# A recommender tower on one core: the second half's gathers wait for the first half's gram

## Chip, core and metric

The kernel runs on one core of a Trainium2 chip. The metric is the device time of one execution in microseconds (us), as the median of several runs; lower is better. The engines are TensorE (PE in the profile; PEld is its weight load), VectorE (DVE), ScalarE (ACT), GpSimd (POOL) and SyncE (SP). DMAs are issued from the queues of SP, ACT and POOL.

## What is computed

For each of 2048 samples, 27 embedding rows of 128 values are looked up in 27 tables, all pairwise dot products of them are taken (351 pairs), and the result goes through three layers with the sample's `r_bottom_mlp_out`:

```python
e = jnp.stack([tbl_0[ids[:, 0]], tbl_1[ids[:, 1]], ..., tbl_26[ids[:, 26]]], axis=1)
interactions = jnp.einsum('bfd,bgd->bfg', e, e)
x = interactions.reshape(B, F * F)[:, TRIL_IDX]      # the 351 entries below the diagonal
z = jnp.concatenate([r_bottom_mlp_out, x], axis=1)
h = jnp.concatenate([z, r_bottom_mlp_out], axis=1)
h = jnp.maximum(h @ W_top1 + b_top1, 0.0)            # 607 -> 512
h = jnp.maximum(h @ W_top2 + b_top2, 0.0)            # 512 -> 256
y = h @ W_top3                                       # 256 -> 1
```

The tables have 1000, 1250, 12500 or (one of them) 125000 rows; everything is float32.

## The kernel before

The samples are cut into 16 **halves** of 128 (`HALVES`), two of which make one tile for the layers. The 27 features of a half come in two ways.

**Ten small tables are looked up on TensorE.** They lie in SBUF, split into a high and a low part (ScalarE L415, VectorE L624, from stages that SP loads at L337). VectorE compares the ids with row numbers and makes one-hot masks (L583, L587), and TensorE multiplies table chunks by masks (L687). One look-up serves up to four halves; the pairs of tables in `OWN` take turns, so that the look-ups behind a half have 32 or 52 matmuls. The results are copied to `eH` (L424, L600) and placed in `eT` (L438).

**Seventeen tables are gathered.** GpSimd issues one indirect DMA for each table and half (L311): 128 rows of 512 bytes into `rows`, which has space for two halves. They are in five groups of 4, 4, 3, 3 and 3 (`GROUPS`, `NG` = 5). Halves 0, 1 and 2 have a sixth, the extra group (`EXTRA`, L322): 2, 2 and 1 gathers that stand in for small tables whose look-up comes too late. TensorE waits for a group's semaphore, transposes its tables (L706), and ScalarE and VectorE copy them into `eT` (L432, L608).

**The gram.** When all groups of half h are in `eT`, TensorE forms the pairwise products with 128 small matmuls (L723) in four sets (`SETS`) over three banks. ScalarE and VectorE copy them to `pairs` (L468, L618), and SP moves them to `x` (L360), from where TensorE takes them in layer 1 (L742, L746); layer 2 is L778, layer 3 L788.

**Order on TensorE**, written out by hand: the front (look-ups 0 to 3 between the transposes of half 0), gram 0, then the look-ups behind it; then for each half h from 1: its transposes, a part of the layers of an earlier tile (two blocks of layer 1 in even halves, layer 2 in odd ones), gram h, the look-ups behind gram h, and in even halves the other two blocks of layer 1. An instruction that waits holds everything behind it on its engine.

**Order on GpSimd**: it waits for the ids, then goes through the halves and, within one, the groups; the extra group of a half stands behind its five. From half 2 on, each group waits until the same group of half h - 2 has been transposed (L304), since its space is used again, and the first group also waits for the end of gram h - 2 (L308). Half 0 and half 1 have neither wait. `gram_full` is counted up by the last matmul of each set; set n of all sets uses bank n % 3.

SP, in its own order: the ids, the small tables (each stage again when the split of an earlier one has been made), hot ids, the weights (L385 to L392), and then for each half the loads for the layers. ScalarE waits for the weights (L519) before it copies the first pairs.

Of the kernel before, what the change touches and what calls it, by code (L numbers as in the profile page):

```python
# [39 lines left out]
SETS = HALF // SET  # L40
# [29 lines left out]
def used(n, b):  # L70

    return (n - b + BANKS - 1) // BANKS
# [53 lines left out]
def transpose_fill(h, g):  # L126
    return NUMBER["transpose", h, g]
# [18 lines left out]
def build(nc, tables, idx_d, hot_ids_d, bottom_d, w1_d, wa_d, wb_d, b1_d, w2_d, b2_d, w3_d, ident_d, rowid_d, out_d):  # L146
# [6 lines left out]
    with ctx:  # L153
# [65 lines left out]
        def rows_of(h, g):  # L219
            first, size = GROUPS[g]  # L220
            return rows[:, h % 2, first * D:(first + size) * D]
# [6 lines left out]
        def extra_row(h, k):  # L228
            at = (h % 2 * len(LATE) + list(LATE).index(k)) * D
            return h1[:, 2:4, :].rearrange("p m s -> p (m s)")[:, at:at + D]  # L230
# [21 lines left out]
        def looked_up(n, k):  # L252

            _, _, wide = LOOKUPS[n]
            first = (WINDOW - wide) * HALF if n < FRONT else 0
            return eH[:, k, first:first + wide * HALF], col_bank[lookup_fill(n, k) % BANKS][:, 0:wide * HALF]
# [10 lines left out]
        def x_block(h, r):  # L267

            (i, n), row = BLOCKS[r], BLOCK_ROW[r]
            c = max(0, 1 - i)  # L270
            return x[row:row + n, h // 2 % 2, h % 2, c * HALF:X_CHUNKS * HALF], \
                pairs[0:n, (i + c - 1) * HALF:(i + X_CHUNKS - 1) * HALF]

        def layer1_out(u, m):

            if u == TILES:
                return (*col_bank, gram_bank[1].rearrange("p q g -> p (q g)"))[m][:, 0:HALF]
            _, at, size = unit_columns(u)
            return mlp_bank[m // 2][:, m % 2, at:at + size]

        def layer2_out(u, m):
            if u == TILES:
                return gram_bank[2].rearrange("p q g -> p (q g)")[:, m * HALF:(m + 1) * HALF]
            _, at, size = unit_columns(u)
            return mlp_bank[0][:, m, at:at + size]
# [9 lines left out]
        @block.gpsimd  # L295
        def _(pool):
            pool.wait_ge(idx_loaded, 16)
            for h in range(HALVES):
                for g, (first, size) in enumerate(GROUPS):
                    before = h * NG + g - RING  # L300
                    if before >= 0:

                        n = transpose_fill(before // NG, before % NG)
                        pool.wait_ge(col_full[n % BANKS], n // BANKS + 1)  # L304
                    if h >= 2 and g == 0:

                        last = (h - 1) * SETS - 1
                        pool.wait_ge(gram_full[last % BANKS], last // BANKS + 1)  # L308
                    for i in range(size):
                        f = first + i  # L310
                        pool.indirect_dma_start(  # L311
                            out=rows_of(h, g)[:, i * D:(i + 1) * D], out_offset=None, in_=tables[GATHERED_TABLES[f]],
                            in_offset=bass.IndirectOffsetOnAxis(ap=idx[:, h * GATHERED + f:h * GATHERED + f + 1], axis=0),
                        ).then_inc(gathered[(h * NG + g) % RING], 16)
                if h < len(EXTRA):
                    if h >= 2:

                        n = transpose_fill(h - 2, NG)
                        pool.wait_ge(col_full[n % BANKS], n // BANKS + 1)
                    for k in EXTRA[h]:  # L320
                        at = HALVES * GATHERED + EXTRA_IDS.index((h, k))
                        pool.indirect_dma_start(  # L322
                            out=extra_row(h, k), out_offset=None, in_=tables[HOT_TABLES[k]],
                            in_offset=bass.IndirectOffsetOnAxis(ap=idx[:, at:at + 1], axis=0),
                        ).then_inc(extra_gathered[h], 16)
            for b in range(BANKS):
                pool.wait_ge(gram_copied[b], STRIPS * used(HALVES * SETS, b))
            for r in range(2, len(BLOCKS), 3):
                out, src = x_block(LAST, r)
                pool.dma_start(out, src).then_inc(last_x_loaded, 16)  # L330
# [555 lines left out]
```

## Time and profile before

| | us |
|---|---|
| median of 3 timed runs | 412.73 (412.5 to 413.49) |
| span of the profiled execution | 563.8 |
| own time of the profiled execution beside its span | none is given |
| mean granted clock of TensorE | 0.845 of full speed |
| TensorE busy / GpSimd busy (profiled) | 395.0 / 292.0 |
| VectorE / ScalarE busy (profiled) | 231.8 / 156.7 |
| moved by DMA | 40.50 MB, mean 72 GB/s |

One execution was profiled, and it was 151 us longer than a timed run. Its rows show durations of single instructions, their order and what released them. In a row, "idle before <-X" is the time that the engine stood before this instruction and what ended the wait; "issue" is time in which the engine waited for nothing that the profile shows; "remote" or "another core or an unknown queue" is a release that the profile can't attribute. PEclk is the clock granted to TensorE, as a share of 2.4 GHz. DMA share is the mean busy share of the core's 16 DMA engines.

### The profile page before, as it was taken

Reading aid. Unit: us, or ns where it says so; the run is one execution under the profiler, and the core shown is the slowest. Engines: PE = TensorE matmul, PEld = TensorE weight load, DVE = VectorE, ACT = ScalarE, POOL = GpSimd, SP = SyncE. Lnnn points to the kernel's source line nnn. Section 1 sums busy time; section 2 is a strip of 40 time slices with the busy share of each in tenths; the row PEclk is TensorE's granted clock in tenths of the full one; section 3 lists DMA queues with packets and bytes.
Section 4 is the critical chain, followed back from the end, with each engine's and each line's share of the span. In section 5 each row is a group of like instructions: output and inputs, shape, how many; then the busy total and the mean of one; then the engine's idle time right before and its main releaser. Section 6 shows DMA issues by size and latency. Waiting matters only on the chain.

```text
span 563.8 us, 9147 instructions
## 1 busy us (share of the span) xinstructions
PE 395.0 (70%) x3669; PEld 336.8 (60%) x3669; DVE 231.8 (41%) x430; ACT 156.7 (28%) x337; POOL 292.0 (52%) x284
## 2 busy tenths in 40 slices
PE   1620868397979578688939587797979490924987
PEld 1520756285868467576737376676857390823977
DVE  3530667073836143373617052472716050422430
ACT  3200543021424142324115042322215041401433
POOL 6776007656574747374735737373746656172010
PEclk9975898688989979699969879697979785885999
DMA  8761272122331312041411212140413111030000
GB/s 212 193 170 47 79 185 70 48 84 66 93 86 29 99 35 74 23 118 34 145 28 62 76 33 72 24 117 24 131 37 75 48 53 51 6 95 19 16 8 9
DMA packets 20737, 40.50 MB, mean 72 GB/s; under 512 B 7128, under 2 KB 11428, under 8 KB 20696
## 3 DMA queue, kind: packets, MB, share of 16 engines
q1 hardware_dynamic: 11674, 21.64, 14.1%
q0 software_dynamic: 8960, 18.22, 12.8%
q8 instruction: 29, 0.48, 0.3%
q14 instruction: 12, 0.10, 0.1%
q10 hardware_dynamic: 62, 0.06, 0.1%
HBM read 36.81 MB, written 0.01 MB: 65 GB/s over the span
## 4 chain that ended last, share of the span: by engine, by line
PE 51%; issue 18%; another core or an unknown queue 11%; DVE 8%; DVEq 3%; ACT 3%; DMA 3%; SPq 1%; ACTq 0%
PE col_bank L687 17%; PE gram_bank L723 15%; PE mlp_bank L778 6%; PE mlp_bank L746 6%; DVE mask L583 4%; PE col_bank L706 4%; DVEq L590 3%; PE mlp_bank L742 2%; DMA b<-in_b 2%; DVE mask L587 2%; ACT eT L438 1%; DMA pairs<-in_tbl 1%; DVE parts L624 1%; DVE eT L608 1%
## 5 line engine op out<-in xcount | busy, mean ns | idle before, releaser
L311 POOL DMA_INDIRECT rows<-in_tbl,idx x272 | 285.5, 1050 | 219.2 <-PE gram_bank L723 138.1
L687 PE MATMUL col_bank<-mask,parts 125*128 125x512 f32 (+3 forms) x768 | 168.0, 381 | 21.8 <-DVE parts L624 12.2
L687 PEld LDWEIGHTS col_bank<-mask,parts 125*128 125x128 f32 x768 | 139.8, 204 | 45.0 <-DVE parts L624 12.1
L583 DVE TENSOR_SCALAR mask<-hot_i,rowid 125x1024 fp32r<-125x1024 int32 (+3 forms) x152 | 103.9, 684 | 65.0 <-remote 30.6
L723 PE MATMUL gram_bank<-eT 128*58 128x52 f32 x2048 | 87.2, 244 | 59.6 <-issue 54.0
L723 PEld LDWEIGHTS gram_bank<-eT 128*58 128x58 f32 x2048 | 78.5, 160 | 71.3 <-issue 67.1
L618 DVE COPY pairs<-gram_bank 26x208 f32<-26x208 f32 x128 | 46.7, 365 | 159.4 <-remote 91.5
L706 PE MATMUL col_bank<-ident,rows 128*128 128x128 f32 x272 | 41.7, 293 | 82.5 <-issue 30.5
L468 ACT ACTIVATE pairs<-gram_bank 26x208 f32<-26x208 f32 x128 | 44.5, 348 | 153.0 <-remote 84.6
L706 PEld LDWEIGHTS col_bank<-ident,rows 128*128 128x128 f32 x272 | 32.4, 149 | 90.7 <-issue 88.4
L424 ACT ACTIVATE eH<-col_bank 128x512 f32<-128x512 f32 (+3 forms) x30 | 15.3, 516 | 148.4 <-issue 59.6
L608 DVE COPY eT<-col_bank 128x384 f32<-128x384 f32 (+2 forms) x42 | 25.1, 611 | 67.3 <-remote 47.0
L746 PE MATMUL mlp_bank<-x,w 126*128 126x256 f32 (+3 forms) x192 | 48.1, 389 | 0.0
L438 ACT ACTIVATE eT<-eH 128x256 f32<-128x256 f32 (+1 forms) x64 | 43.3, 788 | 16.0 <-issue 9.0
L746 PEld LDWEIGHTS mlp_bank<-x,w 126*128 126x128 f32 (+1 forms) x192 | 37.4, 203 | 5.7
L587 DVE TENSOR_SCALAR mask<-hot_i,rowid 125x512 fp32r<-125x512 int32 (+2 forms) x80 | 33.5, 461 | 5.6 <-PE col_bank L687 1.6
L778 PE MATMUL mlp_bank<-h,w 128*128 128x256 f32 (+1 forms) x128 | 35.7, 445 | 0.0
L778 PEld LDWEIGHTS mlp_bank<-h,w 128*128 128x128 f32 x128 | 28.9, 241 | 5.0
L432 ACT ACTIVATE eT<-col_bank 128x384 f32<-128x384 f32 (+2 forms) x41 | 21.7, 553 | 28.6 <-remote 20.2
L742 PE MATMUL mlp_bank<-bottom,w 128*128 128x256 f32 (+1 forms) x64 | 20.6, 405 | 0.0
L477 ACT ACTIVATE h<-mlp_bank,b 128x256 f32<-128x256 f32 (+1 forms) x32 | 13.0, 458 | 26.6 <-remote 20.3
L330 POOL DMA_DIRECT2D x<-pairs x3 | 1.6, 532 | 36.1 <-DVE pairs L618 36.1
(34 smaller groups left out, 83.9 us busy)
## 6 DMA issues: line engine op xcount, KB each, us to landing
hot_i<-in_hot_ids SPq DMA_DIRECT2D x13, 512.0 KB
rows<-in_tbl,idx POOLq DMA_INDIRECT x272
pairs<-in_tbl SPq DMA_DIRECT2D x8, 448.0 KB
hot_i<-in_hot_ids SPq DMA_DIRECT2D x8, 256.0 KB
pairs<-in_tbl SPq DMA_DIRECT2D x2, 560.0 KB
bottom<-in_bottom SPq DMA_DIRECT2D x8, 128.0 KB
hot_i<-in_hot_ids SPq DMA_DIRECT2D x2, 384.0 KB
x<-pairs SPq DMA_DIRECT2D x16, 39.0 KB
```

Of the source, the lines that this page charges most:

```text
L311: pool.indirect_dma_start(out=rows_of(h, g)[:, i * D:(i + 1) * D], out_offset=None, in_=tables[GATHERED_TABLES[f]], in_offset=bass.Indirec ...
L438: return nc.scalar.activation(eT[:, :, first:last].rearrange("p s f -> p f s"), eH[:, first:last, at:at + HALF], ACT.Copy)
L468: last = nc.scalar.activation(pairs_of(s, 1, j), gram_of(n % BANKS, 1, j), ACT.Copy)
L583: last = nc.vector.tensor_scalar(mask[0:ROWS, entry % MASKS, 0:2 * size], ids, row_of(ks[0], c), None, ALU.is_equal)
L587: last = nc.vector.tensor_scalar(mask[0:ROWS, entry % MASKS, i * size:(i + 1) * size], ids, row_of(ks[0], 2 * c + i), None, ALU.is_equal)
L618: last = nc.vector.tensor_copy(pairs_of(s, 0, j), gram_of(n % BANKS, 0, j))
L687: last = nc.tensor.matmul(col_bank[fill % BANKS][:, 0:size], parts[k][0:ROWS, part, c * D:(c + 1) * D], mask[0:ROWS, entry % MASKS, at:at ...
L706: last = nc.tensor.transpose(col_bank[fill % BANKS][:, i * HALF:(i + 1) * HALF], src, ident[:, :])
L723: last = nc.tensor.matmul(gram_bank[n % BANKS][COLUMNS * t:COLUMNS * t + GRAM_ROWS, q, 0:PACK * (F - 1)], eT[:, a:a + PACK, :].rearrange(" ...
L742: nc.tensor.matmul(layer1_out(u, m), w1[:, X_CHUNKS, m * 128:(m + 1) * 128], bottom[:, buf, at:at + size], start=True, stop=False)
L746: last = nc.tensor.matmul(layer1_out(u, m).rearrange("p (h s) -> p h s", s=HALF), w1[0:k, c, m * 128:(m + 1) * 128], x[0:k, buf, at // HAL ...
L778: last = nc.tensor.matmul(layer2_out(u, m), w2[:, c, m * 128:(m + 1) * 128], h1[:, c, at:at + size], start=(c == 0), stop=(c == N1 // 128 ...
```

## The change

GpSimd's wait for a gram stands ahead of half 1 too. For half 1 it is the last set of gram 0; for half 2, which waited for gram 0 before, it is the same wait again, and for the later halves nothing changes. No DMA, no size and no other engine's instructions are changed.

```diff
--- before.py
+++ after.py
@@ -302,9 +302,9 @@
 
                         n = transpose_fill(before // NG, before % NG)
                         pool.wait_ge(col_full[n % BANKS], n // BANKS + 1)
-                    if h >= 2 and g == 0:
-
-                        last = (h - 1) * SETS - 1
+                    if h >= 1 and g == 0:
+
+                        last = max(1, h - 1) * SETS - 1
                         pool.wait_ge(gram_full[last % BANKS], last // BANKS + 1)
                     for i in range(size):
                         f = first + i
```

## Rows read from the trace of the kernel before

**Rows 1.** The page's head: span and instructions.

```profile
span 563.8 us, 9147 instructions
```

**Rows 2.** The page's chain that ended last: shares of the span by engine.

```profile
PE 51%; issue 18%; another core or an unknown queue 11%; DVE 8%; DVEq 3%; ACT 3%; DMA 3%; SPq 1%; ACTq 0%
```

**Rows 3.** Waits, 31 to 54 us: waited for: total, times, longest.

```profile
ACT eH L424 <- issue: 28.8, 1, 28.8
DVE mask L583 <- issue: 9.2, 2, 6.4
```

**Rows 4.** Timeline, TensorE, gram 1: start, us, what [idle before <-releaser].

```profile
102.31 0.34 PE L723 MATMUL gram_bank<-eT 128*58 128x52 f32 x4 [1.11 <-issue]
...
112.26 3.44 PE L723 MATMUL gram_bank<-eT 128*58 128x52 f32 x63 [0.45 <-issue]
```

**Rows 5.** Chain, halves 9, 10 and one gram: start, us, what.

```profile
331.31 7.48 PE col_bank L687 x32
...
347.90 0.93 PE gram_bank L723 x29
...
361.67 12.15 PE col_bank L687 x52
...
381.45 0.46 PE gram_bank L723 x12
...
420.87 3.55 PE gram_bank L723 x128
```

**Rows 6.** Chain, front: shares over 34.6 to 58.05 us; gram 0's end.

```profile
by line: another core or an unknown queue 44.8%; issue 43.2%; DVE mask L583 13.9%; DVEq L590 0.8%
...
82.59 1.84 PE gram_bank L723 x32
```

**Rows 7.** Stretches to gram 0's end: engines busy, PEclk, DMA share, GB/s.

```profile
0.00:28.80 28.80, 11.04 (x51) 10.92 (x52) 12.34 (x20) 7.84 (x9) 20.38 (x23) 1.00 0.79 200
28.80:53.40 24.60, 3.31 (x19) 2.97 (x18) 5.48 (x7) 0.00 (x0) 18.81 (x20) 0.61 0.48 119
53.40:84.40 31.00, 22.20 (x208) 19.30 (x208) 18.03 (x25) 13.90 (x26) 0.03 (x1) 0.83 0.48 122
```

**Rows 8.** Timeline, GpSimd: first and last gather of halves 1, 2, 3.

```profile
29.14 0.94 POOL L311 DMA_INDIRECT rows<-in_tbl,idx  x1 [0.30 <-issue]
...
52.49 0.94 POOL L322 DMA_INDIRECT h<-in_tbl,idx  x1 [0.30 <-issue]
85.22 1.63 POOL L311 DMA_INDIRECT rows<-in_tbl,idx  x1 [31.79 <-PE gram_bank L723]
...
108.92 0.94 POOL L322 DMA_INDIRECT h<-in_tbl,idx  x1 [0.30 <-issue]
116.48 0.94 POOL L311 DMA_INDIRECT rows<-in_tbl,idx  x1 [6.62 <-PE gram_bank L723]
...
138.38 0.94 POOL L311 DMA_INDIRECT rows<-in_tbl,idx  x1 [0.30 <-issue]
```

**Rows 9.** Waits over the whole span, GpSimd's.

```profile
POOL rows L311 <- PE gram_bank L723: 138.1, 14, 31.8
```

**Rows 10.** DMA issues: KB each, median us to landing.

```profile
x<-pairs POOLq DMA_DIRECT2D x1, 16.5 KB, 2.0
```

**Rows 11.** Chain near the end.

```profile
527.71 5.95 PE col_bank L687 x52
...
538.49 0.87 PE col_bank L706 x6
```

**Rows 12.** Timeline, TensorE, from gram 0 to gram 1.

```profile
84.36 9.62 PE L687 MATMUL col_bank<-mask,parts 125*128 125x512 f32 x32
...
97.65 0.38 PE L706 MATMUL col_bank<-ident,h 128*128 128x128 f32 x2
98.66 0.55 PE L723 MATMUL gram_bank<-eT 128*58 128x52 f32 x13 [0.63 <-DVE eT L608]
```

**Rows 13.** The stretch with TensorE's long stop.

```profile
32.00:54.00 22.00, 0.11 (x2) 0.00 (x0) 3.97 (x6) 0.27 (x1) 16.56 (x17) 0.55 0.51 126
```

## The prediction, made before the change was run

> **What bounds the kernel now.** Read first how far the profile can be trusted in length. The page gives a span of 563.8 us [rows 1], while the timed runs have a median of 412.73 us, 151 us less; no own time of the profiled execution is given beside its span. The chain that ended last names the surplus: "issue" holds 18% and "another core or an unknown queue" 11% of the span [rows 2], and 29% of 563.8 us is 164 us, close to 151. So I take nearly all of that idle time to belong to the profiled execution alone. What it looks like: in the first stretch ScalarE stood still for 28.8 us and VectorE for 9.2 us in two waits, with nothing named but "issue" [rows 3], and in the gram of half 1 TensorE paused for about 1 us every few matmuls while GpSimd gathered, then ran 63 of them in 3.44 us once it had stopped [rows 4]. The same 128 matmuls without these pauses take 3.55 us [rows 5].
>
> Next, take them out of the front. I call T the end of gram 0: 82.59 + 1.84 = 84.4 us in the profile. Between 34.6 and 58.05 us the chain has 44.8% + 43.2% of such pieces, which of 23.45 us is 20.6 us [rows 6]. That puts T in a timed run near 63.8 us. The DMA rates by stretch are the check [rows 7]: 28.8 x 200 + 24.6 x 119 + 31.0 x 122 thousand bytes are 12.5 MB by T, which at the first stretch's 200 GB/s are 62 us. The front is thus close to what the queues moved at their fastest.
>
> Then the steady part, and here two engines are almost level. **GpSimd**: one gather is 0.94 us with 0.30 us before it, and up to 1.63 us beside VectorE's masks [rows 8]. Eighteen of them take 85.22 to 109.86 us, 24.6 us; seventeen 116.48 to 139.32 us, 22.8 us, so 23.1 us to the start of the next set if it never waits. **TensorE** without pauses: half 9 is 16.6 us from the first of its 32 look-up matmuls (331.31) to the gram's start (347.90), with 3.55 us of gram 20.1 us; half 10, with 52 look-ups, is 19.8 us (361.67 to 381.45), with the gram 23.3 us [rows 5]; the mean is 21.7 us. So a gather set (23.1) is longer than TensorE's half (21.7). In the profile GpSimd looks slack, waiting 138.1 us for the gram in 14 waits [rows 9], but only because TensorE's halves were stretched to some 31 us there.
>
> Does GpSimd's row of gathers give the timed total? From T: 0.8 us to wake (84.43 to 85.22), 24.9 us for half 2's, 13 x 23.1 = 300.3 us for halves 3 to 15, about 2.0 us for the last to land (a GpSimd DMA of 16.5 KB landed in 2.0 us [rows 10]), and 25.3 us from the last transposes at 538.5 us to the end of the span [rows 11]. Together 353.3 us; with T = 63.8 that is 417 us, 1% above the median. The same by TensorE: 17.8 us to the end of gram 1 (gram 1 began 14.2 us after T [rows 12], and 3.55), 13 x 21.7 = 282 us, and 36.1 us from 527.7 to the end [rows 11], 336 us in all, 400 us with T. The gathers fit better, so I take GpSimd as the bound after gram 0, with between 0 and some 10 us of slack.
>
> **The change part by part.** Nothing is removed. The 17 gathers of half 1 and, behind them on the same engine, the 2 of its extra group now wait for gram 0; halves 2 and later wait for what they waited for. Before, the 19 began at 29.14 us and ended at 53.43 us, and GpSimd was idle for 31.8 us from there to gram 0 [rows 8]. Queued behind the waiting instruction are all later gathers, and nothing else; nobody but TensorE's transposes waits for them. SP's queue isn't touched.
>
> First term, **the gathers added behind T**: 19 x 24.9 / 18 = 26.3 us. Everything of GpSimd after T moves back by this.
>
> Second, how it shows at TensorE. Its order is fixed: 32 look-ups, transposes of half 1, gram 1. The gram began at T + 14.2 us. It now begins when the nineteenth gather has landed and been transposed and copied: 0.8 + 26.3 + 2.0 + about 1.3 (from the extra group's transposes, after 97.4, to the gram at 98.66 us [rows 12]) = T + 30.4 us, 16.2 us late. Half 2 waits again: its 18 gathers end at 0.8 + 26.3 + 24.9 = 52.0, land at 54, while TensorE, free of gram 1 at 34, has 12.2 us of look-ups [rows 5] and stands from 46 to 54. Before, gram 1 ended at 17.8 and the look-ups at 30, so that transposing began there and ended at 33: half 2 is 21 us late. From then on the lag can only grow, because 23.1 is more than 21.7: up to the full 26.3 us if GpSimd was the bound before, and no less than these 16 to 21 us if it wasn't. So the loss lies between 16 (only gram 1's delay) and 26; I take 26.3 less 2 us for slack, since the sum for GpSimd was over the median and leaves little: **+24.3 us**.
>
> By the Trainium skill ("DMA: Bandwidth & Descriptors", section on the anatomy of one SWDGE DMA) a DMA from GpSimd has some 2.0 us of fixed cost, most of it waiting for the write's receipt. The nearest row here is the closing DMA's 2.0 us, and agrees [rows 10].
>
> Third, **the front gets lighter**. The 19 gathers move 64 KB each (128 rows of 512 B), 1.25 MB, which at 200 GB/s are 6.2 us of the queues' time. If the queues alone set T, it falls by 6.2; if the chain of table load, split, mask and look-up sets it, by 0, since those gathers stand on no step of that chain and the DMA share was 0.48 while they ran [rows 7]. I take **-3 us**.
>
> Fourth, TensorE now idles about 15 us before gram 1 and 8 us before half 2's transposes. After 22 us without a matmul its granted clock was 0.55 of 2.4 GHz over 32 to 54 us [rows 13], where it had been 1.00 before [rows 7]: part of that time at 1.2 GHz. Gram 1 and the 12.2 us of look-ups behind it may cost up to 6 us more at half clock, but behind them TensorE waits 8 us for half 2's gathers anyway. So 0, and +3 at most if the second idle slows half 2 too and GpSimd isn't the bound.
>
> **Sum**: +24.3 - 3 + 0 = +21.3 us. 412.7 + 21.3 = **434.0 us**.
>
> **The rivals.** (1) *Cheap delay.* Outside the profile a gather takes nearer 1.0 us than 1.3 us, because its 0.30 us gap or its contention is the profile's. Then 19 cost 19 us, gram 1 begins at 0.8 + 19 + 2.0 + 1.3 = 23.1, 8.9 us late, half 2's 18 land at 39.8 against look-ups ending near 38.9, and a set of 17 us never binds again: +10 with -3 is 420 us. Against it: the gap is 0.30 us at every gather, long before other engines are busy, and TensorE alone gives only 400 us. (2) *Full price or more.* GpSimd was the bound without slack and the front gives nothing: +26.3, with the clock's +3, 442 us. (3) *The other side, faster: the gathers hold up the front.* VectorE, ScalarE and TensorE stood from about 32 to 53.4 us, and ScalarE's wait of 28.8 us ended, by the rows, as the last of the gathers that the change moves had been made [rows 3, 8]. If that stop is real in part in timed runs, moving them frees it. By the Trainium skill ("Runtime: NRT & Kernel Launch", section on instruction fetch) each engine's sequencer fetches its instructions over its own DMA queue, mostly hidden; the profile lists such queues, but no row here shows a fetch that was late. Its price: up to 20.6 us of front [rows 6] against +24.3 us, and it decides for faster from the point where more than the loss is freed, that is with a loss at its lower end of 16: 412.7 + 16 - 20.6 = 408 us. Against it: with a front of 84 us the timed total would leave 328 us for a rest that takes 336 by TensorE alone. (4) *Nothing happens*: the wait is passed at once. Against it: GpSimd gets there at about 28.8 us and gram 0 ends at 84.4 in the profile [rows 6, 8]. A time unchanged would need 19 gathers that are hidden beside the look-ups, which is 9.6 us of cover for 26.3 [rows 12].
>
> **How the numbers follow.** The forecast, between 424 and 439 us: 0.64. Cheap delay, 416 to 424: 0.15. Full price, 439 to 445: 0.10. Front freed: 0.08, of which 0.05 comes out faster by over 0.3%, 0.02 within it. Nothing happens: 0.03, within it. A difference of 0.3% (1.2 us) is about what a measurement of this kernel can tell from none. The range goes from 418 us, with most of the cheap case, to 441 us. Faster 0.05, same 0.05, slower 0.90.
>
> **What would show it.** In the profile of the changed kernel GpSimd stands from about 28.8 us to the end of gram 0, then issues 37 gathers without a pause, half 1's first. If the stops in the profile go with gathers, TensorE's and ScalarE's stop after 32 us is shorter there and gram 0 ends well before 84 us, which by itself says little of the timed runs. The transposes of half 1 come at the gathers' pace, the first pieces of wait naming the DMA or GpSimd, and gram 1 begins some 30 us behind gram 0. I'm wrong if gram 1 follows gram 0 within 20 us, if GpSimd has long waits for the gram in a run whose halves are as short as the timed ones, or if T is far from 64 us in timed runs.

## The result, and the profile after

| | before | changed |
|---|---|---|
| median of the timed runs, us | 412.62 (411.54 to 413.49, 4 runs) | 433.65 (433.18 to 434.73, 4 runs) |
| ratio, 95% interval | | 1.051 (1.0484 to 1.0536) |
| span of the profiled execution, us | 563.8 | 431.4 |

The change costs 21.0 us, 5.1%. The profile of before, at 563.8 us, shows a condition with stops, in which the kernel before took about 575 us in one later set of 17 runs too; the timed runs of this table were free of it. So the kernel before was profiled once more (the first experiment below), at 410.3 us, and the comparison is made with that.

The waits on GpSimd of the changed kernel, over the whole span (waited for: us in total, times, longest), answer [rows 9]:

```profile
POOL rows L311 <- PE gram_bank L723: 25.8, 4, 24.9
```

and its timeline answers [rows 8]: the first gather of half 1, the last of its extra group, the first of half 2, the last of half 2's group and the last of all.

```profile
55.45 1.29 POOL L311 DMA_INDIRECT rows<-in_tbl,idx  x1 [24.88 <-PE gram_bank L723]
...
80.42 0.95 POOL L322 DMA_INDIRECT h<-in_tbl,idx  x1 [0.30 <-issue]
81.67 0.95 POOL L311 DMA_INDIRECT rows<-in_tbl,idx  x1 [0.30 <-issue]
...
105.05 0.95 POOL L322 DMA_INDIRECT h<-in_tbl,idx  x1 [0.30 <-issue]
...
403.00 0.95 POOL L311 DMA_INDIRECT rows<-in_tbl,idx  x1 [0.30 <-issue]
```

GpSimd stands 24.9 us for the end of gram 0 and then issues its 258 remaining gathers in one row, 347.6 us from start to start: 1.35 us each. What TensorE does meanwhile is seen in its own timeline of the changed kernel, which answers [rows 12]:

```profile
53.33 1.84 PE L723 MATMUL gram_bank<-eT 128*58 128x52 f32 x32 [4.17 <-ACT pairs L468]
55.10 9.45 PE L687 MATMUL col_bank<-mask,parts 125*128 125x512 f32 x32
64.39 0.60 PE L706 MATMUL col_bank<-ident,rows 128*128 128x128 f32 x4
69.14 0.96 PE L706 MATMUL col_bank<-ident,rows 128*128 128x128 f32 x4 [4.15 <-DMA rows<-in_tbl,idx]
72.90 0.90 PE L706 MATMUL col_bank<-ident,rows 128*128 128x128 f32 x3 [2.80 <-DMA rows<-in_tbl,idx]
...
84.18 4.65 PE L723 MATMUL gram_bank<-eT 128*58 128x52 f32 x128 [0.63 <-issue]
...
114.32 3.62 PE L723 MATMUL gram_bank<-eT 128*58 128x52 f32 x128
```

From the second group on, the transposes of half 1 come one group at a time, each released by a gather's landing, and gram 1 begins at 84.18, 29 us after gram 0's end at 55.2. The page's chain that ended last, which answers [rows 2], now has GpSimd in it with 30%:

```profile
PE 43%; POOL 30%; issue 11%; DMA 6%; DVE 4%; DVEq 2%; SPq 2%; ACT 1%; ACTq 0%; POOLq 0%
```

### The profile page after: what moved, and what is told of

Same layout as the page of the kernel before. It is cut to its first block, busy times and chain, and to the rows that moved or that the text cites. A ratio compares the mean times of both kernels' runs of the same rounds, so it can differ in the third digit from the quotient of the medians.

```text
span 431.4 us, 9147 instructions
## 1 busy us (share of the span) xinstructions
PE 364.3 (84%) x3669; PEld 310.2 (72%) x3669; DVE 231.0 (54%) x430; ACT 156.6 (36%) x337; POOL 293.8 (68%) x284
## 4 chain that ended last, share of the span: by engine, by line
PE 43%; POOL 30%; issue 11%; DMA 6%; DVE 4%; DVEq 2%; SPq 2%; ACT 1%; ACTq 0%; POOLq 0%
POOL rows L311 29%; PE col_bank L687 15%; PE mlp_bank L746 8%; PE gram_bank L723 8%; PE mlp_bank L778 4%; PE mlp_bank L742 3%; PE col_bank L706 3%; DMA rows<-in_tbl,idx 3%; DVE mask L583 3%; DVEq L590 2%; DMA b<-in_b 2%; DMA pairs<-in_tbl 1%; PE mlp_bank L788 1%; POOL h L322 1%; DVE mask L587 1%
## 5 line engine op out<-in xcount | busy, mean ns | idle before, releaser
L687 PE MATMUL col_bank<-mask,parts 125*128 125x512 f32 (+3 forms) x768 | 164.7, 375 | 16.3 <-DVE mask L583 16.3
L687 PEld LDWEIGHTS col_bank<-mask,parts 125*128 125x128 f32 x768 | 136.3, 199 | 39.3 <-DVE parts L624 14.8
L468 ACT ACTIVATE pairs<-gram_bank 26x208 f32<-26x208 f32 x128 | 44.3, 346 | 93.0 <-PE gram_bank L723 76.5
L723 PEld LDWEIGHTS gram_bank<-eT 128*58 128x58 f32 x2048 | 57.8, 136 | 11.9 <-issue 7.6
L723 PE MATMUL gram_bank<-eT 128*58 128x52 f32 x2048 | 60.0, 220 | 6.4 <-ACT pairs L468 4.2
L746 PE MATMUL mlp_bank<-x,w 126*128 126x256 f32 (+3 forms) x192 | 52.1, 413 | 0.0
L746 PEld LDWEIGHTS mlp_bank<-x,w 126*128 126x128 f32 (+1 forms) x192 | 41.0, 222 | 7.4
L778 PE MATMUL mlp_bank<-h,w 128*128 128x256 f32 (+1 forms) x128 | 27.4, 367 | 0.0
L778 PEld LDWEIGHTS mlp_bank<-h,w 128*128 128x128 f32 x128 | 22.6, 190 | 2.5
L742 PE MATMUL mlp_bank<-bottom,w 128*128 128x256 f32 (+1 forms) x64 | 23.5, 455 | 0.0
L624 DVE TENSOR_TENSOR parts<-pairs,parts 125x1024 fp32r<-125x1024 f32 (+1 forms) x10 | 12.5, 1276 | 11.2 <-ACT parts L415 10.8
```

The costliest lines, as they stand in the source:

```text
L468: last = nc.scalar.activation(pairs_of(s, 1, j), gram_of(n % BANKS, 1, j), ACT.Copy)
L687: last = nc.tensor.matmul(col_bank[fill % BANKS][:, 0:size], parts[k][0:ROWS, part, c * D:(c + 1) * D], mask[0:ROWS, entry % MASKS, at:at ...
L723: last = nc.tensor.matmul(gram_bank[n % BANKS][COLUMNS * t:COLUMNS * t + GRAM_ROWS, q, 0:PACK * (F - 1)], eT[:, a:a + PACK, :].rearrange(" ...
L742: nc.tensor.matmul(layer1_out(u, m), w1[:, X_CHUNKS, m * 128:(m + 1) * 128], bottom[:, buf, at:at + size], start=True, stop=False)
L746: last = nc.tensor.matmul(layer1_out(u, m).rearrange("p (h s) -> p h s", s=HALF), w1[0:k, c, m * 128:(m + 1) * 128], x[0:k, buf, at // HAL ...
L778: last = nc.tensor.matmul(layer2_out(u, m), w2[:, c, m * 128:(m + 1) * 128], h1[:, c, at:at + size], start=(c == 0), stop=(c == N1 // 128 ...
```

## The experiments

Times of experiments stand beside a kernel before that ran on the same chip; ratios are to that.

**1. The kernel before, once more** (no edit).

> The kernel before, unchanged, profiled once more: the first profile was 151 us longer than a timed run, this one is wanted without those stops. Theory (after gram 0 GpSimd's gathers are the bound): gram 0 ends near 59.6 us, some 4 us later than in the changed kernel, GpSimd's 239 gathers of halves 2 to 15 then follow each other with hardly a wait for a gram (under 5 us in all behind the first), and the span is about 410. Rival (TensorE is the bound in the kernel before, and only the transposes' waiting costs in the changed one): GpSimd waits for the gram in most halves, 10 us or more in sum behind the first, and gram 0 ends earlier than 59.

Measured: 412.3 us, span 410.3. Its timeline of TensorE, from gram 0 to gram 2:

```profile
47.87 2.77 PE L723 MATMUL gram_bank<-eT 128*58 128x52 f32 x96 [2.05 <-ACT eT L438]
57.34 1.85 PE L723 MATMUL gram_bank<-eT 128*58 128x52 f32 x32 [6.70 <-ACT pairs L468]
59.11 8.44 PE L687 MATMUL col_bank<-mask,parts 125*128 125x512 f32 x32
...
72.30 3.62 PE L723 MATMUL gram_bank<-eT 128*58 128x52 f32 x128 [0.63 <-DVE eT L608]
...
97.95 3.62 PE L723 MATMUL gram_bank<-eT 128*58 128x52 f32 x128
```

and of GpSimd, the last gather of half 1's extra group, the first of half 2 and the last of all:

```profile
55.97 0.94 POOL L322 DMA_INDIRECT h<-in_tbl,idx  x1 [0.30 <-issue]
59.97 1.62 POOL L311 DMA_INDIRECT rows<-in_tbl,idx  x1 [3.06 <-PE gram_bank L723]
...
382.72 0.95 POOL L311 DMA_INDIRECT rows<-in_tbl,idx  x1 [0.30 <-issue]
```

Gram 0 ends at 59.2 us, 4.0 us later than in the changed kernel, and none of the long stops of [rows 3, 4] is there. GpSimd's whole wait for grams is 4.0 us, 3.06 of it for gram 0: the 138.1 us of [rows 9] came from the stops on TensorE. The 239 gathers from half 2 on take 322.8 us from start to start, 1.36 us each. So GpSimd's row runs without a break in both kernels, and the last gather begins at 382.72 before and 403.00 after, 20.3 us apart.

The chain that ended last alone would not have shown this. In this profile of the kernel before it names TensorE, and GpSimd with 6% only:

```profile
PE 66%; DVE 9%; DMA 7%; POOL 6%; issue 4%; DVEq 3%; SPq 2%; ACT 2%; ACTq 0%
```

With two engines this close, a chain that passes from one to the other says little about which of them sets the time; experiment 5 tries it.

**2 and 3. Moving fewer gathers behind gram 0.** In the second only the two of the extra group wait, in the third the wait stands ahead of half 1's fourth group (8 gathers behind it).

```diff
# experiment 2, ahead of the loop over EXTRA[h]
+                    if h == 1:
+                        last = SETS - 1
+                        pool.wait_ge(gram_full[last % BANKS], last // BANKS + 1)
# experiment 3
-                    if h >= 2 and g == 0:
+                    if h >= 2 and g == 0 or h == 1 and g == 3:
-                        last = (h - 1) * SETS - 1
+                        last = max(1, h - 1) * SETS - 1
```

> Only the two gathers of half 1's extra group wait for gram 0; half 1's 17 go early as before. Theory (each gather moved behind gram 0 adds its 1.35 us, less its share of the front, 0.23 us): 2 x 1.12 = +2.2 us, 414.8 us. Rival (a few gathers behind gram 0 are hidden by the 9.6 us of look-ups there): 412.6 us, no change.

Measured: 415.06 us beside 413.58, ratio 1.0042 (1.0024 to 1.006), that is +1.0 to +2.5 us.

> The wait stands ahead of half 1's fourth group: 11 gathers go early, 6 and the 2 extra ones wait for gram 0. Theory: 8 x 1.12 = +9.0 us, 421.6 us. Rival (hidden by the look-ups behind gram 0): the eighth lands at 0.3 + 10.8 + 3 = 14 us behind gram 0, when TensorE's transposes reach it anyway, so 413 to 414 us.

Measured: 422.28 us, ratio 1.0201 (1.0165 to 1.0237), +6.8 to +9.8 us. With 2, 8 and 19 gathers moved the cost is about 1.7, 8.3 and 21.0 us, 0.9 to 1.1 us each, so the look-ups behind gram 0 hide nothing of them. The timeline of GpSimd in the third, first gather behind the wait and last of all:

```profile
57.51 1.29 POOL L311 DMA_INDIRECT rows<-in_tbl,idx  x1 [13.08 <-PE gram_bank L723]
...
391.90 0.94 POOL L311 DMA_INDIRECT rows<-in_tbl,idx  x1 [0.30 <-issue]
```

The last gather begins 9.2 us later than in the kernel before.

**4. No gram waits at all.**

```diff
-                    if h >= 2 and g == 0:
-
-                        last = (h - 1) * SETS - 1
-                        pool.wait_ge(gram_full[last % BANKS], last // BANKS + 1)
```

> GpSimd's wait for a gram is taken out of all halves; a group still waits until the same group two halves earlier has been transposed. Theory: half 2's gathers follow half 1's at about 54 us and no longer wait for gram 0 near 59.6, so the row of gathers moves forward by about 5 us: 407 to 408 us. Rival (TensorE is the bound): no change, 412.6 us, or slower, since these gathers then run beside the loads of the weights that gram 0 waits for.

Measured: 411.18 us beside 413.58, ratio 0.994 (0.9911 to 0.9969): faster by 1 to 4 us, less than forecast. The expectation had the end of half 1's gathers from [rows 8], 53.4 us; in the profile of experiment 1, without stops, these gathers run beside a busier VectorE and DMA (DMA share 0.86 from 28.8 us to gram 0's end, where [rows 7] have 0.48), and end at 56.9 us. So only 2 to 3 us of wait were there to be had: half 2's first gather begins at 57.77 in place of 59.97 us, the last of all at 380.95 in place of 382.72.

**5 and 6. Fourteen gathers fewer**, in the kernel before (5) and in the changed one (6). The last table of the fifth group isn't gathered from half 2 on, so one feature keeps the rows of halves 0 and 1.

```diff
-                    for i in range(size):
+                    for i in range(size - 1 if h >= 2 and g == NG - 1 else size):
# and in gathered_count
-        return 16 * sum(GROUPS[k % NG][1] for k in range(n % RING, n + 1, RING))
+        return 16 * sum(GROUPS[k % NG][1] - (k // NG >= 2 and k % NG == NG - 1) for k in range(n % RING, n + 1, RING))
```

> The kernel before with one gather fewer in each half from half 2 on (14 in all): the last table of the fifth group keeps its old rows, so the features of one table are not those of its ids. TensorE waited 11.4 us for gathers in the clean profile of the kernel before. Theory (GpSimd's row is the bound, TensorE close behind): the 14 gathers are worth 14 x 1.35 = 18.9 us, of which only TensorE's 11.4 us can be had, so 401 to 403 us. Rival (TensorE's chain sets the time before the change): 412.6 us, hardly a change.

Measured: 396.8 us beside 413.07, ratio 0.9594 (0.9545 to 0.9643), span 395.1. That is 16.3 us off, more than the 11.4 us that TensorE had waited. The 11.4 us were read from the wrong rows. A transpose begins with its weight load, and it is the weight loads that stand longest for a gather; in the kernel before, profiled again (waited for: us in total, times, longest), they have 14.5 + 1.2 = 15.7 us, near the 16.3:

```profile
PEld col_bank L706 <- DMA rows<-in_tbl,idx: 14.5, 9, 3.1
...
PEld col_bank L706 <- DMA h<-in_tbl,idx: 1.2, 1, 1.2
```

In experiment 5 all that is left of them is one row:

```profile
PEld col_bank L706 <- DMA h<-in_tbl,idx: 0.2, 1, 0.2
```

> The same 14 gathers left out of the changed kernel. Theory: there GpSimd's row has 26 us more behind gram 0 and stays the bound throughout, so nearly all of the 18.9 us comes off: 433.7 - 18.9 = 414.8 us. Rival (the change costs its time once, at gram 1 and half 2, and TensorE's chain rules from there): most of the 21 us stays over the kernel before with the same gathers left out, which gives 430 us if that one is at 412, and anything above 420 speaks for it.

Measured: 417.26 us, ratio 1.0092 (1.0056 to 1.0128); by the ratios (1.051 - 1.0092) that is 17.2 us under the changed kernel, where 18.9 were forecast. Its last gather begins at 385.95 in place of 403.00 us, 17.1 us earlier. Here TensorE still waits for gathers (us in total, times, longest):

```profile
PEld col_bank L706 <- DMA rows<-in_tbl,idx: 21.3, 8, 4.9
PE col_bank L706 <- DMA rows<-in_tbl,idx: 18.8, 7, 4.6
```

So gathers are what the time behind gram 0 is made of, in both kernels. Once they are fewer, TensorE bounds the one from before, at 396.8 us, with GpSimd close behind (its last gather begins 16.0 us earlier and its row still has hardly a break), and GpSimd still bounds the changed one. The rival that the change costs once, at gram 1, and that TensorE rules from there, wanted over 420 and is out.

**7. GpSimd idle in the front instead of behind it.** Half 1's gathers wait for the transposes of half 0's extra group.

```diff
+                    if h == 1 and g == 0:
+                        n = transpose_fill(0, NG)
+                        pool.wait_ge(col_full[n % BANKS], n // BANKS + 1)
```

> Half 1's gathers wait, but for an earlier event: the transposes of half 0's extra group, near 38 us, where GpSimd comes by at 30 us. Its idle time of 7 to 8 us is then in the front. Theory (time off GpSimd's row costs as soon as it uses up the 3.1 us that GpSimd waited for gram 0): half 2's gathers begin at 63 to 64.5 us in place of 60.0, so +3 to +4.5 us: 415.5 to 417 us. Rival (gathers cost only if they are issued behind gram 0, where look-ups and masks run): 412.6 us, or less by the front's relief.

Measured: 418.01 us beside 413.07, ratio 1.0119 (1.0094 to 1.0144), +4.9 us. The timeline of GpSimd, the first gather of half 1 and the first of half 2:

```profile
37.70 1.17 POOL L314 DMA_INDIRECT rows<-in_tbl,idx  x1 [9.92 <-PE col_bank L709]
...
66.35 1.51 POOL L314 DMA_INDIRECT rows<-in_tbl,idx  x1 [0.30 <-issue]
```

The idle time was 9.9 us rather than 7 to 8, and half 2's row begins 6.4 us later than before and its last gather 4.2 us later (386.93 us), so the numbers are over the forecast by the same cause. Idle time of GpSimd in the front costs too, beyond the 3 us that it had to spare. The rival of the expectation, that only gathers issued behind gram 0 cost, isn't excluded by this run: gram 0 ends at 57.9 us here, and five of half 1's gathers begin behind it, which at the 0.9 to 1.1 us of experiments 2 and 3 would be 4.5 to 5.5 us. In a row without gaps the two ways of counting give nearly the same sum.

**8 to 12. Gram 0 earlier.** ScalarE waits for the weights ahead of its first copies of pairs, which hold up gram 0's last set (57.34 above, released by "ACT pairs L468"). The wait is moved to the first use of a weight:

```diff
-            act.wait_ge(weights_loaded, 16 * WEIGHT_LOADS)
...
                 if u == 0 and b == 0:
+                    act.wait_ge(weights_loaded, 16 * WEIGHT_LOADS)
                     act.wait_ge(w1_summed, 1)
```

It was run in the changed kernel (8), in the kernel before (9), and there together with experiment 4's edit (10).

> The changed kernel, with ScalarE's wait for the weights moved from ahead of its first copies of pairs (in which gram 0's last set is held up until 53.3 us) to the first use of a weight. Gram 0 then ends near 51 us in place of 55.2. Theory (the row of GpSimd's gathers starts with the end of gram 0 and sets the total): 4 us less, 429.5 us. Rival (the total hangs on something of TensorE's or of the DMA queues behind gram 0): under 1 us less, 433 us.

> The same edit in the kernel before. Gram 0 would end near 52 us, but GpSimd is busy with half 1's gathers until about 57 us, so only its wait of 3.1 us for gram 0 can go. Theory: 1.5 to 3 us less, 410 to 411 us, as without the gram waits. Rival (an earlier gram 0 is worth the same in both kernels): 7 us less, 406 us.

> The kernel before with both edits: the late wait for the weights and no gram waits on GpSimd. Theory: GpSimd never waits in either, so the two edits don't add up: 410 to 411 us. Rival (each has its own gain): 408 us.

In these three the kernel before itself took 575.2 us (560.7 to 584.1, 17 runs), and they tell nothing of the forecasts; what they do show stands in the last section. Measured were 576.8 us (8), 570.8 us (9; 544.5 to 577.1 in 12 runs) and 667.9 us (10). By the medians that is 1.003, 0.992 and 1.161 of the kernel before. Set against the lowest three of its 17 runs (560.7 to 567.1 us), 8 has a ratio of 1.0137 (1.004 to 1.0234) and 10 one of 1.1753 (1.1668 to 1.1838); 9 stays unclear. So 8 and 9 were run once more:

> The changed kernel with the late wait for the weights once more, for a comparison beside a kernel before at about 413 us; that at 575 us didn't test the theory. Theory: gram 0 ends near 51 us in place of 55.2 and GpSimd's row of gathers with it: 4 us less than the changed kernel, 429.5 us, a ratio of 1.041 to the kernel before where the changed kernel has 1.051. Rival: 433 us, a ratio of 1.049 or more. Should the kernel before take 575 us again: a ratio of 1.00 to 1.02, as in the first run.

Measured: 429.28 us beside 413.45, ratio 1.0382 (1.0332 to 1.0433). The timeline of GpSimd, first gather of half 1, last of its extra group, last of all:

```profile
51.43 1.29 POOL L311 DMA_INDIRECT rows<-in_tbl,idx  x1 [20.74 <-PE gram_bank L723]
...
76.70 0.94 POOL L322 DMA_INDIRECT h<-in_tbl,idx  x1 [0.30 <-issue]
...
399.62 0.94 POOL L311 DMA_INDIRECT rows<-in_tbl,idx  x1 [0.30 <-issue]
```

> The kernel before with the same edit, once more for the same reason. Theory: only GpSimd's 3.1 us of wait for gram 0 can go, 410 to 411 us, a ratio of 0.993 to 0.996. Rival (an earlier gram 0 is worth the same in both kernels): 406 us, 0.983. Should the kernel before take 575 us again: no change beyond the scatter there.

Measured: 410.87 us, ratio 0.9941 (0.9917 to 0.9964). The same edit, which ends gram 0 at about 51.2 us in both, is worth 4.4 us in the changed kernel by the medians (433.65 to 429.28) and 5.3 us by the ratios to the kernel before (1.051 to 1.0382), and 2.4 to 2.6 us in the kernel before. In the one the row of gathers begins with gram 0's end, 51.43 in place of 55.45 us, and its last gather is 3.4 us earlier; in the other only GpSimd's 3 us of wait go.

Experiments 4 and 12 both beat the kernel before, by about 0.6%, and, as far as the waits show, by the same 3 us of GpSimd's time. Both together were run only in the set at 575 us, so whether they add up in the other condition stays open.

## Why the prediction was right

The time came out at 433.65 us for 434.0, and the steps held one by one, with one belief behind them that did not. That it came so close is luck: the lag behind gram 0 was 25.1 us for 24.3 and the front's gain 4.0 us for 3, and the two errors cancel.

- **GpSimd is the bound after gram 0**: right. It was chosen because its sum came nearer to the median than TensorE's. With the measured 59.2 us for T the two sums are 412.5 us for GpSimd and 395 us for TensorE. The spans that answer them are 410.3 us for the kernel before and 395.1 us for experiment 5, where TensorE hardly waits for a gather. GpSimd's terms erred both ways: half 2's 18 gathers took 26.2 us where the sum has 24.9, and those of halves 3 to 15 took 297.5 us (86.15 to 383.67) where it has 300.3.
- **T = 63.8 us**: 59.2 measured. Taking only the named pieces out of the chain left too much: in the clean profile gram 0's first set already begins at 47.87 us. The DMA check, 62 us at 200 GB/s, was nearer, since the queues moved 216 GB/s from 28.8 us to T.
- **The gathers added, +26.3 us**: half 1's first to half 2's first are 81.67 - 55.45 = 26.2 us.
- **Gram 1 16.2 us late** against gram 0: 29.0 us behind it where it was 13.1, 15.9 us late. **Half 2, 21 us**: gram 2 begins 59.1 us behind gram 0's end in place of 38.8, 20.4 us late. From there the lag grew to 25.1 us (21.1 us of span and 4.0 of front), as "up to 26.3" said; taken were 24.3. On GpSimd half 2's first gather is 25.7 us late against gram 0 and the last of all 24.3; the rest comes behind the last gather, which the span outlasts by 28.4 us where it was 27.6.
- **The front, -3 us** of 0 to 6.2: -4.0. The last load of the weights, which gram 0's last set waits for through ScalarE, was under way for 11.72 us before and 9.68 us after, and began 2.0 us earlier. The chains of the kernel before, profiled again, and then of the changed one:

```profile
44.85 11.72 DMA b<-in_b
```

```profile
42.88 9.68 DMA b<-in_b
```

With 8 gathers moved (experiment 3) gram 0 ended at 57.2 us, with 19 at 55.2, 0.2 to 0.25 us a gather, under the 0.33 us that a gather's 64 KB take at 200 GB/s. That the shared queues are the cause is argued from this slope; no run changed the queues' load by itself.
- **The clock, 0**: gram 1 took 4.65 us in place of 3.62, at a granted clock of 0.76 where it was 1.00 before, and half 2's layer 1 blocks 6.6 us (107.77 to 114.32) in place of 4.3 us, at 0.55, near the level of 1.2 GHz, where it was 0.83. That is 3.3 us together; the "up to 6 us" of the prediction has no working. It cost nothing in the end: gram 2 and gram 3 both begin 20.4 us later against gram 0 than before, then TensorE waits for gathers again (1.8 us at 155.39 us), and gram 4 is 25.3 us late. Ahead of gram 1 TensorE mostly waited, and the mean clock of that stretch was 0.68. The stretch's row in the changed kernel (start:end, us, busy time of PE, PEld, DVE, ACT, POOL, then clock, DMA share, GB/s):

```profile
55.20:84.20 29.00, 14.16 (x53) 10.08 (x54) 11.24 (x17) 4.88 (x10) 22.34 (x22) 0.68 0.23 61
```

- **The step that failed** is the first: that the idle time of "issue" and "another core" belonged to the profiled execution alone. Another profiled execution of the same kernel took 410.3 us (experiment 1), and timed executions of one whole set were as long as the first profile, 560.7 to 584.1 us. The consequence drawn from it, to leave the stops out of the sum, was right for the runs that were asked for, but for a reason that the profile could not give.
- **The rivals.** Cheap delay fell with the pace of 1.35 us outside the first profile too, and full price with the front's 4.0 us. The rival on the other side, that the gathers hold up the front, is no fancy: it happens in the condition with stops (below), where the total gains nothing by it. Without them the front gained 4.0 us, the queues' share.

## What to carry to other kernels

An engine that looks half idle in a profile may be the bound of the timed runs, when the profile is longer than they are and the others are stretched in it: compare each engine's own row, back to back, with the timed total before its waits are believed. If a queue of equal pieces feeds the whole rest of a kernel, put no idle time ahead of it: every microsecond in which it stands beyond its slack comes back at the end, here 21 of 26, however much cover the next few steps seem to give.

## What the runs showed that was not expected

The kernel before has a second condition, in which it takes 560.7 to 584.1 us in a whole set of 17 runs, and 563.8 us in the profile of [rows 1]. In it the other engines stop, mostly while GpSimd gathers. The front shows it best, because experiments 8 and 9 differ there only in where half 1's gathers are. TensorE in 9, with half 1's gathers in the front (31.11 to 55.38 us), before gram 0:

```profile
38.84 0.49 PE L706 MATMUL col_bank<-ident,rows 128*128 128x128 f32 x3
58.58 1.62 PE L706 MATMUL col_bank<-ident,rows 128*128 128x128 f32 x6 [19.25 <-issue]
...
71.37 3.62 PE L723 MATMUL gram_bank<-eT 128*58 128x52 f32 x128 [1.56 <-ACT eT L438]
```

and in 8, with them behind gram 0:

```profile
42.65 1.39 PE L706 MATMUL col_bank<-ident,rows 128*128 128x128 f32 x9
...
53.89 3.62 PE L723 MATMUL gram_bank<-eT 128*58 128x52 f32 x128 [1.55 <-ACT eT L438]
...
89.39 0.25 PE L723 MATMUL gram_bank<-eT 128*58 128x52 f32 x1 [0.21 <-issue]
90.12 0.34 PE L723 MATMUL gram_bank<-eT 128*58 128x52 f32 x1 [0.48 <-issue]
```

Without gathers there is no stop of 19 us, and gram 0 begins 17.5 us earlier; the stops come back at gram 1, which is now beside the gathers. There the change costs little or nothing that these runs can tell: the medians are 576.8 us in 8 and 570.8 us in 9, which differ by the change alone, and 9's runs scatter over 33 us. And there the gram waits on GpSimd are worth much: without them (experiment 10) the time was 667.9 us, 17.0% more than in 9, where leaving them out gained 0.6% in the other condition. The time is lost in the grams. TensorE's waits in them that name nothing but "issue", in 9 and in 10 (us in total, times, longest):

```profile
PE gram_bank L723 <- issue: 51.4, 58, 1.9
```

```profile
PE gram_bank L719 <- issue: 175.6, 170, 2.6
```

In 10 one half's 17 gathers run from 99.47 to 120.58 us and the gram beside them from 104.38 us on, a few matmuls at a time; then 52 of its matmuls follow each other in 2.86 us:

```profile
123.46 2.86 PE L719 MATMUL gram_bank<-eT 128*58 128x52 f32 x52 [0.99 <-issue]
```

What puts a set of runs into this condition, and by what path gathers stop the other engines, no run here shows. The experiments' runs of 544 us and more were all on one chip and those of 394 to 430 us on three others, so the chip is a possible cause that stays untested. The load of the DMA queues doesn't tell the two conditions apart: they moved 207 GB/s in 9's long stop (39.4 to 58.5 us) and 216 GB/s from 28.8 us to gram 0's end in experiment 1, where no such stop is. The Trainium skill ("Runtime: NRT & Kernel Launch", section on instruction fetch mechanics) has each sequencer fetch its instructions over its own DMA queue while it executes, mostly hidden; stops that carry only "issue" would fit a fetch that isn't hidden, but no run here shows a late one: the traces don't time the fetches, and the packets of the larger instruction queue, 0.48 MB in both, took 0.3% of the DMA engines' time over 563.8 us and 0.5% over 410.3 us.
